# Decoder layer on one core: weights centred first, four weight sums on VectorE, a new order of the front

## The chip, the cores and the metric

The kernel runs on one core of one Trainium2 chip. The metric is the device time in microseconds (us) of one execution; lower is better. Engines are called as the profile calls them: PE (TensorE), DVE (VectorE), ACT (ScalarE), POOL (GpSimd) and SP (SyncE, which issues all DMAs here). A line such as L1070 is that line of the kernel's file.

## What is computed

One decoder layer over 8 sequences ("batches") of 512 tokens with 256 features, in float32. Three sublayers, each on a layer norm of x and added to x:

- A, self attention with one head of 128: softmax(Q Kᵀ / sqrt(128)) V, times a mask over the head's dimension, times w_o.
- B, cross attention with a context: relu(x̂ Wᵀ + b) against relu(ctx Wᵀ + b), masked keys out, softmax, times ctx.
- C, a gated FFN of 1024 with quantised products: activations are rounded to 8 bits per token, weights to -1, 0, 1 by the mean of |w| of each of the three matrices, out = down(silu(gate(x̂)) * up(x̂)).

The reference, cut:

```
x = x + attn(layernorm(x), head_dim_mask, w_q, w_k, w_v, w_o)
x = x + xattn(layernorm(x), ctx, mask, W, b)
scale = 1 / clip(mean(|w|), 1e-5);  w3 = clip(round(w * scale), -1, 1) / scale
x = x + bitlinear(silu(bitlinear(xn, w_gate)) * bitlinear(xn, w_up), w_down)
```

## The kernel before

Nothing loops over the work in order: five lists, PE_ORDER, ACT_ORDER, DVE_ORDER, POOL_ORDER and SP_ORDER, hold the steps of each engine one after the other, and every engine runs its list, each step waiting on counting semaphores for what it needs. An entry is stream.step/batch. Streams: W and F prepare weights (F those of the FFN), E is the context's projection (YP), A, B and C are the sublayers, S are loads and stores on SP. So a step that waits holds all that stand behind it in its engine's list, and a load that waits on SP holds the later loads.

Products are made in fp32r pieces: a tensor is split into a high part (a copy by ACT, `hi`) and a low part (source minus high part, by DVE or POOL, `lo`), and PE does hi*hi, hi*lo, lo*hi (product3, L1070 to L1072). Batch 0 of stream A uses plain float32 products instead, on copies of Q, K, V (L1080, L1125, L1139).

Steps of A for a batch: bn, ag (DVE: statistics of x), rs (POOL: reciprocal deviation), xT (ACT hi and POOL lo of the transposed x), Q, K, V (PE, then copies), VT (transposed V), S0 to S3 (scores of 128 queries; DVE multiplies them by the deviations and takes the maximum, L1479), N (its negative), exp (ACT, L867), P0 to P3 (PE transposes of the exponentials, copied as hi and lo), H (times V), Y0, Y1 (times w_o; DVE adds to x). Of batch 0 the deviations come through W.rs (DVE) and W.r (PE, then ACT's copy of r); DVE's V step (L1491) and S steps need that copy. From batch 1 on they go to DRAM and come back spread over the partitions (SP steps S.rw, S.rb).
The weights of Q, K, V are centred by their column means instead of centring x: W.sumQ/K/V on PE (L1317), then centreQ/K/V on DVE (L1614), in place; W.qkv (ACT) and W.split (DVE) make their hi and lo parts for batches 1 to 7.
Steps of B: norm (ACT), XT0, XT1 (PE transposes, hi on ACT, lo on DVE), XP0, XP1 (projection; relu on ACT, lo on POOL), S, exp, P, O (DVE adds to x), ctx (hi on ACT, lo on POOL), mask (ACT turns the loaded bytes into float, L905, which DVE adds to the scores).
Steps of C: bn, ag, rs, sh, norm, mx, sc, rc, xq (quantising; xq on POOL), S.xqT (a transposing DMA from SP), g0 to g7 and u0 to u7 (PE, L1284), t (ACT tanh), u (ACT copy), G (gate on DVE, product on POOL), hm, hs, hr, hq, hb, S.hT (transposing DMA), DN (PE, L1304).

The weights of the FFN are prepared once: F.gate, F.up, F.down load 1 MB each; F.sum0 to F.sum5 sum |w| over halves of gate (0, 1), up (2, 3), down (4, 5), all on ACT (L859, Abs with an accumulator); F.total (PE) adds over the partitions; F.sc0 to F.sc3 (DVE) make the scales; F.round (POOL) and F.sign (ACT) make the -1, 0, 1. B.XT1/0 waits for F.sc0, as they use one bank.

PSUM banks of stream A are dealt out by a_tables: each step of the front takes the next bank of a written list and waits until what was in it has been read. SECOND_BANKS are those of A_NEXT, the end of batch 1; from batch 2 on A takes a0 and a1 in turn and YP takes e.

Of the kernel before, what the change touches and what calls it, by code (L numbers as in the profile page):

```python
# [79 lines left out]
DVE_DN = [(n, t) for n in range(8) for t in range(4) if (n, t) not in POOL_DN]  # L80
SILU = [(6, j) for j in range(4, 8)] + [(7, j) for j in range(8)]
# [8 lines left out]
    E.YP1/3 A.Y0/2 A.Y1/2 C.g0/0 C.u0/0 A.Q/3 B.S0/1 B.S1/1 C.g1/0 C.u1/0 B.P0/1 B.S2/1 C.u2/0 C.g2/0 A.K/3  # L90
    A.V/3 B.P1/1 C.u3/0 C.g3/0 B.O0/1 B.S3/1 B.P2/1 C.g4/0 C.u4/0 E.YP0/4 C.g5/0 B.O1/1 C.u5/0 B.P3/1 B.O2/1
    A.VT/3 A.S0/3 B.O3/1 C.g6/0 C.u6/0 E.YP1/4 B.XT0/2 B.XT1/2 C.g7/0 C.DN0/0 C.u7/0 A.S1/3 A.P0/3 B.XP0/2
    B.XP1/2 A.S2/3 C.DN1/0 C.u0/1 C.g0/1 A.P1/3 A.S3/3 B.S0/2 B.S1/2 C.g1/1 C.u1/1 B.P0/2 B.S2/2 C.DN2/0 C.g2/1
    C.u2/1 C.DN3/0 B.P1/2 B.O0/2 A.P2/3 A.P3/3 C.g3/1 C.u3/1 B.S3/2 B.P2/2 C.g4/1 A.H/3 B.O1/2 B.P3/2 C.u4/1
# [1629 lines left out]
```

## Time and profile before

| | us |
|---|---|
| median of 3 runs | 372.09 |
| lowest and highest run | 371.5, 402.81 |
| the profiled execution | 372.06 |
| its span, first to last instruction | 370.1 |
| busy in it: PE, PEld, DVE, ACT, POOL | 361.5, 280.2, 313.8, 318.6, 294.0 |

The span is that of the instructions of one profiled execution; its own time has 1.96 us around them. In a timeline each row has start and length in us, engine, line, operation, the tile written and the tiles read, and the count where instructions are merged; brackets hold the idle time before it and what ended it. Matmuls overlap, so the start of the next one says more than the length.

### The profile page before, as it was taken

The numbers are of one execution on the slowest core, as the hardware profiler recorded it, in microseconds if no ns is written. First come the engines' busy times: TensorE is split into PE (matmuls) and PEld (weight loads), VectorE is DVE, ScalarE is ACT, GpSimd is POOL, SyncE is SP. The second block draws the span as 40 slices with busy tenths as digits, with TensorE's granted clock in tenths as the row PEclk, the third lists the DMA queues.
The fourth block names the chain that finished last, engine by engine and source line by source line (L and its number), as shares of the span: only waits on it lengthen the run. The fifth ranks groups of instructions, "written<-read, shape, count | busy, mean of one in ns | idle before, by whom it ended". The sixth has DMA issues, their size and how long they took to land.

```text
span 370.1 us, 7362 instructions
## 1 busy us (share of the span) xinstructions
PE 361.5 (98%) x2116; PEld 280.2 (76%) x2116; DVE 313.8 (85%) x918; ACT 318.6 (86%) x590; POOL 294.0 (79%) x421
## 2 busy tenths in 40 slices
...
DMA packets 47735, 36.92 MB, mean 100 GB/s; under 512 B 39248, under 2 KB 40912, under 8 KB 47312
## 3 DMA queue, kind: packets, MB, share of 16 engines
...
## 4 chain that ended last, share of the span: by engine, by line
PE 76%; POOL 6%; ACT 5%; DMA 4%; DVE 3%; issue 3%; SPq 1%; POOLq 0%; ACTq 0%; DVEq 0%
PE b_bank L1070 8%; PE b_bank L1071 8%; PE b_bank L1072 8%; PE a_bank L1070 6%; PE a_bank L1072 6%; PE a_bank L1071 6%; PE g_bank L1284 5%; PE d_bank L1304 5%; PE u_bank L1284 5%; PE b_bank L1212 3%; DMA x_all<-in_x 2%; PE a_bank L1132 2%; PE b_bank L1183 2%; POOL c_work L703 1%; POOL xp_lo L656 1%
## 5 line engine op out<-in xcount | busy, mean ns | idle before, releaser
L703 POOL TENSOR_TENSOR c_work<-c_work 128x512 f32<-128x512 f32 x48 | 61.8, 1297 | 3.4 <-DVE c_work L1540 2.4
L960 ACT ACTIVATE c_work<-g_bank,c_tanh_scale 128x512 f32<-128x512 f32 x52 | 35.9, 690 | 5.8 <-PE g_bank L1284 3.3
L1070 PE MATMUL b_bank<-ctx_hi,b_pT_hi 128*128 128x256 f32 x128 | 39.2, 307 | 0.0
L1540 DVE SCALAR_TENSOR_TENSOR c_work<-c_work,g_bank 128x512 f32<-128x512 f32 x50 | 33.9, 678 | 6.1 <-ACT c_work L960 5.7
L1071 PE MATMUL b_bank<-ctx_lo,b_pT_hi 128*128 128x256 f32 x128 | 36.1, 282 | 0.0
L1072 PE MATMUL b_bank<-ctx_hi,b_pT_lo 128*128 128x256 f32 x128 | 36.0, 282 | 0.0
L963 ACT ACTIVATE c_work<-u_bank 128x512 f32<-128x512 f32 x48 | 28.9, 601 | 8.2 <-PE u_bank L1284 8.2
L1284 PE MATMUL g_bank<-gateT,xqT 128*128 128x512 bf16 x112 | 33.6, 382 | 0.9 <-ACT xqT L935 0.5
L750 POOL TENSOR_SCALAR c_work<-c_work,h_q 128x1024 f32<-128x1024 f32 x28 | 31.7, 1132 | 3.2 <-DVE h_q L1574 3.2
L1284 PE MATMUL u_bank<-upT,xqT 128*128 128x512 bf16 x112 | 33.5, 381 | 0.6 <-DVE c_work L1535 0.6
L1567 DVE TENSOR_REDUCE h_max<-c_work 128x1 f32<-128x1024 f32 x26 | 31.4, 1206 | 1.1 <-POOL c_work L703 1.1
L1304 PE MATMUL d_bank<-downT,c_half 128*128 128x256 bf16 x240 | 31.2, 273 | 0.2 <-DMA c_half<-c_half 0.2
L1304 PEld LDWEIGHTS d_bank<-downT,c_half 128*128 128x128 bf16 x240 | 22.7, 98 | 8.5 <-issue 2.7
L651 POOL TENSOR_TENSOR yp_lo<-e_relu,yp_hi 128x512 fp32r<-128x512 f32 x16 | 20.7, 1295 | 10.2 <-ACT yp_hi L889 10.2
L970 ACT ACTIVATE c_half<-c_work 128x1024 bf16<-128x1024 f32 x26 | 27.3, 1056 | 0.5 <-POOL c_work L750 0.5
L1070 PE MATMUL b_bank<-yp_hi,xp_hi 128*128 128x512 f32 x64 | 27.4, 429 | 0.1
L1070 PEld LDWEIGHTS b_bank<-ctx_hi,b_pT_hi 128*128 128x128 f32 x128 | 24.3, 190 | 1.8 <-issue 0.2
L643 POOL TENSOR_TENSOR a_xT_lo<-a_xT_raw,a_xT_hi 128x512 fp32r<-128x512 f32 x14 | 18.4, 1316 | 8.6 <-ACT a_xT_hi L844 8.6
L1072 PE MATMUL b_bank<-yp_hi,xp_lo 128*128 128x512 f32 x64 | 25.2, 394 | 0.0
L898 ACT ACTIVATE b_p<-b_p,b_nmax 128x512 f32<-128x512 f32 x32 | 23.1, 723 | 2.5 <-DVE b_nmax L1516 2.4
L1071 PE MATMUL b_bank<-yp_lo,xp_hi 128*128 128x512 f32 x64 | 25.1, 391 | 0.0
L1516 DVE CUSTOM_DVE_ANT_0 b_p<-b_bank,mask_add 128x512 f32<-128x512 f32 x32 | 21.8, 683 | 3.7 <-PE b_bank L1072 3.6
...
## 6 DMA issues: line engine op xcount, KB each, us to landing
ctx_raw<-in_ctx SPq DMA_DIRECT2D x8, 512.0 KB, 4.5
a_xT_raw<-in_x_t SPq DMA_DIRECT2D x7, 512.0 KB, 4.4
ctxT_raw<-in_ctx_t SPq DMA_DIRECT2D x7, 512.0 KB, 5.4
x_all<-in_x SPq DMA_DIRECT2D x7, 512.0 KB, 3.8
out<-x_all SPq DMA_DIRECT2D x7, 512.0 KB, 2.9
...
c_work<-in_w_gate SPq DMA_DIRECT2D x1, 1024.0 KB, 10.9
c_work<-in_w_up SPq DMA_DIRECT2D x1, 1024.0 KB, 12.6
```

Of the source, the lines that this page charges most:

```text
L703: pool.tensor_tensor(h[:, t % 2, half * HALF:(half + 1) * HALF], th[:, j % 2, :], up[:, j % 2, :], ALU.mult).then_inc(hs, 1)
L750: pool.tensor_scalar(h_tile(t, n), h_tile(t, n), h_q[:, t:t + 1], ROUND if n < LAST else ROUND_F16, ALU.mult, ALU.add).then_inc(h_rounds, 1)
L960: act.activation(gate_tile(j, n), gu_bank("g", j, n), ACT.Silu if (n, j) in SILU else ACT.Tanh, scale=c_tanh_scale[:, j // 2:j // 2 + 1]). ...
L963: act.activation(up[:, j % 2, :], gu_bank("u", j, n), ACT.Copy).then_inc(ups, 1)
L970: act.activation(h_q8[:, t % 2, :], h_tile(t, n), ACT.Copy, bias=-ROUND).then_inc(hqs, 1)
L1070: pe.matmul(dst, l_hi, r_hi, start=first, stop=False)
L1071: pe.matmul(dst, l_hi, r_lo, start=False, stop=False)
L1072: return pe.matmul(dst, l_lo, r_hi, start=False, stop=last)
L1284: mm = pe.matmul(dst, xqT[:, t * DC + c, :], w[:, c, cols], start=c == 0, stop=c == DC - 1)
L1304: mm = pe.matmul(dn_bank(t, n)[:, 0:D], h_T[:, t % 2, f, :], downT[:, f, :], start=f == 0, stop=f == FC - 1)
L1540: dve.scalar_tensor_tensor(gate_tile(j, n), gate_tile(j, n), 1.0, gu_bank("g", j, n), ALU.add, ALU.mult).then_inc(gates, 1)
L1567: dve.tensor_reduce(h_max[:, one], h_tile(t, n), AX.X, ALU.max, apply_absolute_value=True).then_inc(h_maxes, 1)
```

## The change

1. On DVE all three centrings stand ahead of the statistics of batch 0; K's copy stands ahead of W.split and W.rs.
2. On PE A.S0/0 and A.S1/0 stand ahead of W.r, and E.YP1/0 directly behind E.YP0/0.
3. On SP the load of x of batch 1 goes ahead of W.o, xT/1 and ctxT/1; the mask of batch 0 is loaded behind all weights and S.rw/1, the mask of batch 1 behind S.xqT0/0 and S.ctxT/4. Other loads change places too.
4. F.sum2 to F.sum5 run on DVE (tensor_reduce of absolute values), with a semaphore of their own; ACT keeps F.sum0 and F.sum1.
5. Q and K of batch 2 ("batch three") run before P2 and P3 of batch 1 ("batch two") on PE, in banks e and b0.
6. The lists of all five engines are new up to about the middle of batch 0's FFN, and as before from there: A.S1/3 on PE, B.XT0/2 on ACT, A.N1/3 on DVE, C.G1/1 on POOL, S.hT1/0 on SP.

```diff
-A_NEXT = "S3/1 P1/1 P2/1 P3/1 H/1 Y0/1 Y1/1"
+A_NEXT = "S3/1 P1/1 Q/2 P2/1 K/2 P3/1 H/1 Y0/1 Y1/1"
...
-SECOND_BANKS = ["u", "d", "a0", "a1", "g", "u", "d"]
+SECOND_BANKS = ["u", "d", "e", "a0", "b0", "a1", "g", "u", "d"]
...
+    later = [entry for entry in later if entry not in A_NEXT.split()]
...
+DVE_SUMS = [2, 3, 4, 5]
+ACT_SUMS = [m for m in range(6) if m not in DVE_SUMS]
...
 PE_ORDER = """
-    W.sumQ/0 W.sumK/0 W.sumV/0 A.Q/0 A.K/0 A.V/0 W.r/0 E.YP0/0 A.S0/0 A.S1/0 A.VT/0 A.S2/0 A.S3/0 E.YP1/0 A.P0/0
-    A.P1/0 A.Q/1 A.P2/0 A.K/1 A.P3/0 A.V/1 E.YP0/1 A.H/0 A.VT/1 A.S0/1 A.S1/1 A.Y0/0 E.YP1/1 A.S2/1 A.P0/1
-    A.Y1/0 A.S3/1 A.P1/1 F.total/0 A.P2/1 A.P3/1 E.YP0/2 A.H/1 B.XT0/0 B.XT1/0 E.YP1/2 A.Y0/1 B.XP0/0 B.XP1/0
-    A.Y1/1 A.Q/2 A.K/2 B.S0/0 B.S1/0 A.V/2 B.P0/0 B.S2/0 A.VT/2 B.P1/0 A.S0/2 B.O0/0 B.S3/0 A.S1/2 B.P2/0 B.O1/0
...
+    W.sumQ/0 W.sumK/0 W.sumV/0 A.Q/0 A.K/0 A.V/0 A.S0/0 A.S1/0 W.r/0 E.YP0/0 E.YP1/0 A.VT/0 A.S2/0 A.S3/0 A.P0/0
+    A.P1/0 A.Q/1 A.P2/0 A.K/1 A.P3/0 A.V/1 E.YP0/1 A.H/0 A.VT/1 A.S0/1 A.S1/1 A.Y0/0 A.S2/1 E.YP1/1 A.P0/1
+    A.Y1/0 A.S3/1 A.P1/1 A.Q/2 A.P2/1 A.K/2 A.P3/1 F.total/0 E.YP0/2 A.H/1 B.XT0/0 B.XT1/0 E.YP1/2 B.XP0/0
+    B.XP1/0 A.Y0/1 A.Y1/1 A.V/2 B.S0/0 B.S1/0 A.VT/2 B.P0/0 B.S2/0 A.S0/2 B.P1/0 B.O0/0 A.S1/2 A.P0/2 B.S3/0
...
+    B.XP1/1 E.YP1/3 A.Y0/2 A.Y1/2 C.g0/0 C.u0/0 B.S0/1 B.S1/1 C.g1/0 C.u1/0 A.Q/3 B.P0/1 C.g2/0 C.u2/0 B.S2/1
...
 ACT_ORDER = """
-    A.Q/0 W.qkv/0 W.hi/0 A.xT0/1 E.ctxT/1 A.xT1/1 W.r/0 E.YP0/0 A.VT/0 W.wo/0 F.sum0/0 A.exp0/0 A.exp1/0
-    A.exp2/0 E.YP1/0 A.exp3/0 A.P0/0 A.Q/1 A.P2/0 A.K/1 F.sum1/0 F.sum2/0 E.YP0/1 A.xT0/2 A.xT1/2 F.sum3/0 A.H/0
-    A.VT/1 F.sum4/0 F.sum5/0 A.exp0/1 E.YP1/1 A.P0/1 E.ctxT/2 A.exp1/1 A.exp2/1 A.exp3/1 A.P1/1 A.P2/1 A.P3/1
-    B.mask/0 E.YP0/2 B.norm0/0 B.norm1/0 A.H/1 B.XT0/0 B.XT1/0 B.ctx/0 F.sign0/0 F.sign1/0 B.XP0/0 B.XP1/0
...
+    A.Q/0 W.qkv/0 W.hi/0 W.r/0 A.xT0/1 A.xT1/1 E.YP0/0 A.exp0/0 A.VT/0 A.exp1/0 E.ctxT/1 A.exp2/0 A.exp3/0
+    E.YP1/0 A.P0/0 A.Q/1 A.P2/0 A.K/1 W.wo/0 F.sum0/0 E.YP0/1 A.xT0/2 A.xT1/2 B.mask/0 A.H/0 A.VT/1 F.sum1/0
+    B.ctx/0 A.exp0/1 A.exp1/1 E.YP1/1 E.ctxT/2 A.exp2/1 A.P0/1 A.P1/1 A.Q/2 A.exp3/1 A.P2/1 A.K/2 A.P3/1
+    B.norm0/0 B.norm1/0 E.YP0/2 B.XT0/0 B.XT1/0 A.H/1 E.ctxT/3 B.XP0/0 B.XP1/0 F.sign0/0 F.sign1/0 F.sign2/0
...
+    B.XT1/1 E.YP0/3 F.sign4/0 F.sign5/0 A.H/2 B.XP0/1 B.XP1/1 C.norm1/0 B.ctx/1 B.mask/1 C.t0/0 E.ctxT/4 C.u0/0
...
 DVE_ORDER = """
-    W.centreQ/0 W.centreK/0 A.bn0/0 A.bn1/0 A.ag0/0 A.ag1/0 W.centreV/0 W.split/0 W.rs/0 A.K/0 W.lo/0 W.wo0/0
-    A.bn0/1 A.bn1/1 A.V/0 A.ag0/1 A.S0/0 A.S1/0 A.N0/0 A.N1/0 A.ag1/1 W.wo1/0 A.S2/0 A.S3/0 A.N2/0 A.N3/0
-    A.inv/0 A.P1/0 A.Q/1 A.K/1 A.P3/0 A.V/1 A.H/0 A.S0/1 A.N0/1 A.VT/1 A.S1/1 A.Y0/0 B.bn0/0 A.N1/1 A.S2/1
...
+    W.centreQ/0 W.centreK/0 W.centreV/0 A.bn0/0 A.bn1/0 A.ag0/0 A.ag1/0 A.K/0 W.split/0 W.rs/0 A.bn0/1 A.bn1/1
+    A.ag0/1 A.V/0 A.S0/0 A.S1/0 A.N0/0 W.lo/0 A.N1/0 W.wo0/0 A.ag1/1 A.S2/0 A.S3/0 A.N2/0 A.N3/0 F.sum2/0 A.P1/0
+    A.Q/1 A.K/1 A.P3/0 W.wo1/0 F.sum3/0 F.sum4/0 A.V/1 F.sum5/0 A.H/0 A.inv/0 A.S0/1 A.VT/1 A.N0/1 A.S1/1 A.N1/1
+    A.Y0/0 A.S2/1 A.N2/1 B.bn0/0 A.Y1/0 A.S3/1 B.ag0/0 B.bn1/0 A.N3/1 A.P0/1 A.P1/1 A.Q/2 B.ag1/0 A.P2/1 A.K/2
+    A.P3/1 B.sh0/0 B.sh1/0 A.bn0/2 A.bn1/2 A.ag0/2 A.ag1/2 A.bn0/3 F.sc0/0 F.sc1/0 F.sc2/0 F.sc3/0 A.inv/1
...
 SP_ORDER = """
-    W.qkv/0 W.t0/0 W.t1/0 W.x0/0 W.x1/0 W.o/0 W.W/0 W.c/0 S.xT/1 S.ctxT/1 S.mask/0 S.x/1 F.gate/0 F.up/0
-    F.down/0 S.rw/1 S.xT/2 S.rb/1 S.ctxT/2 S.x/2 S.x/3 S.mask/1 S.mask/2 S.ctx/0 S.rw/2 S.xT/3 S.rb/2 S.ctxT/3
-    S.rw/3 S.ctx/1 S.ctxT/4 S.xqT0/0 S.xqT1/0 S.xT/4 S.rb/3 S.ctx/2 S.ctxT/5 S.hT0/0 S.hT1/0 S.xqT0/1 S.hT2/0
...
+    W.qkv/0 W.t0/0 W.t1/0 W.x0/0 W.x1/0 W.W/0 W.c/0 S.x/1 W.o/0 S.xT/1 S.ctxT/1 F.gate/0 F.up/0 F.down/0 S.xT/2
+    S.rw/1 S.mask/0 S.ctx/0 S.rb/1 S.ctxT/2 S.x/2 S.x/3 S.ctxT/3 S.rw/2 S.rb/2 S.ctx/1 S.xT/3 S.xqT0/0 S.ctxT/4
+    S.mask/1 S.xqT1/0 S.rw/3 S.rb/3 S.ctx/2 S.ctxT/5 S.mask/2 S.hT0/0 S.xT/4 S.hT1/0 S.xqT0/1 S.hT2/0 S.hT3/0
...
@@ act @@
             def prep_sum(j):
                 act.wait_ge(ffn_loaded[j // 2], 16)
-                if j > 0:
-                    act.wait_ge(w_sums, j)
+                if ACT_SUMS.index(j) > 0:
+                    act.wait_ge(w_sums, ACT_SUMS.index(j))
...
@@ pe @@
-                    pe.wait_ge(w_sums, 6)
+                    pe.wait_ge(w_sums, len(ACT_SUMS))
+                    pe.wait_ge(dve_w_sums, len(DVE_SUMS))
...
@@ dve @@
+            def prep_sum(j):
+                dve.wait_ge(ffn_loaded[j // 2], 16)
+                dve.tensor_reduce(w_sum[:, j % 2, j // 2:j // 2 + 1], ffn_raw[j // 2][:, (j % 2) * F:(j % 2 + 1) * F], AX.X, ALU.add,
+                                  apply_absolute_value=True).then_inc(dve_w_sums, 1)
```

## Rows read from the trace of the kernel before

**Rows 1.** The page, part 1: busy time, share of the span, instructions
```profile
...
PE 361.5 (98%) x2116; PEld 280.2 (76%) x2116; DVE 313.8 (85%) x918; ACT 318.6 (86%) x590; POOL 294.0 (79%) x421
...
```

**Rows 2.** Waits of PE, 0 to 50: us in total, times, longest
```profile
...
PE d_bank L1132 <- ACT a_p L867: 1.1, 1, 1.1
PE u_bank L1116 <- DVE vT L1491: 1.0, 1, 1.0
...
PE b_bank L1322 <- DVE vT L1367: 0.5, 1, 0.5
PE g_bank L1070 <- DVE a_pT_lo L1464: 0.4, 1, 0.4
```

**Rows 3.** Windows: length, busy us by engine, clock, DMA share, GB/s
```profile
...
10.00:20.00 10.00, 8.50 (x23) 3.51 (x22) 7.50 (x22) 6.46 (x13) 7.20 (x8) 1.00 1.02 419
...
43.50:86.00 42.50, 42.45 (x245) 36.68 (x246) 31.44 (x110) 37.17 (x68) 30.84 (x38) 1.00 0.27 74
...
340.00:370.10 30.10, 25.98 (x201) 17.63 (x199) 25.27 (x69) 25.61 (x45) 22.82 (x48) 1.00 0.38 106
...
```

**Rows 4.** Timeline of DVE, 0 to 50
```profile
...
8.82 0.46 DVE L1614 SCALAR_TENSOR_TENSOR b_p<-u_bank,b_p 128x128 f32<-128x128 f32 x2
...
11.66 0.68 DVE L1450 COPY upT<-a_bank 128x512 f32<-128x512 f32 x1
...
15.32 1.41 DVE L1355 BATCH_NORM_STATS2 a_bn<-x_all 128x6 f32<-128x256 f32 x4 [2.31 <-DMA x_all<-in_x]
...
32.88 0.69 DVE L1468 TENSOR_TENSOR hT_lo<-d_bank,hT_hi 128x512 fp32r<-128x512 f32 x1 [4.57 <-ACT hT_hi L838]
...
```

**Rows 5.** Chain that ended last, 6 to 16: start us, us, what
```profile
...
6.19 9.11 DMA x_all<-in_x
...
```

**Rows 6.** Tile mask_u, 0 to 50: its loads, issue to landing
```profile
...
DMA to landing us min/median/max: 3.4/3.7/7.9
```

**Rows 7.** Timeline of PE: start, length in us, instruction, idle before
```profile
...
22.09 0.48 PE L1070 MATMUL d_bank<-a_xT_hi,wqkv_hi 128*128 128x512 f32 x1
...
23.56 0.60 PE L1132 MATMUL a_bank<-ident,a_p 128*128 128x128 f32 x4
...
28.61 3.60 PE L1139 MATMUL d_bank<-x_all,downT 128*128 128x512 f32 x8
...
39.74 0.63 PE L1132 MATMUL d_bank<-ident,a_p 128*128 128x128 f32 x4 [1.05 <-ACT a_p L867]
...
43.55 0.47 PE L1070 MATMUL g_bank<-a_pT_hi,b_pT_hi 128*128 128x512 f32 x1 [0.38 <-DVE a_pT_lo L1464]
...
85.80 0.60 PE L1284 MATMUL g_bank<-gateT,xqT 128*128 128x512 bf16 x2
...
```

**Rows 8.** Timeline of ACT, 25 to 50
```profile
...
34.46 1.06 ACT L859 ACTIVATE gateT<-c_half 128x1024 f32<-128x1024 f32 x1
...
35.52 0.71 ACT L867 ACTIVATE a_p<-a_p,a_nmax 128x512 f32<-128x512 f32 x1
...
36.22 0.67 ACT L888 ACTIVATE e_relu<-a_bank,wo_and_small 128x512 f32<-128x512 f32 x1
...
37.36 0.59 ACT L831 ACTIVATE a_pT_hi<-a_bank 128x512 fp32r<-128x512 f32 x1
37.84 1.06 ACT L919 ACTIVATE ctxT_hi<-ctxT_raw 128x1024 fp32r<-128x1024 f32 x1
38.79 0.72 ACT L867 ACTIVATE a_p<-a_p,a_nmax 128x512 f32<-128x512 f32 x1
...
```

**Rows 9.** Groups of DVE by form: count, busy us, mean ns, idle before
```profile
...
L1567 DVE TENSOR_REDUCE h_max<-c_work 128x1 f32<-128x1024 f32 x26 | 31.4, 1206 | 1.1 <-POOL c_work L703 1.1
...
```

**Rows 10.** The page, part 6: DMA issues, KB each, us to landing
```profile
...
ctxT_raw<-in_ctx_t SPq DMA_DIRECT2D x7, 512.0 KB, 5.4
...
c_work<-in_w_up SPq DMA_DIRECT2D x1, 1024.0 KB, 12.6
```

**Rows 11.** Timeline of SP, 0 to 60
```profile
...
5.70 0.44 SPq L550 DMA_DIRECT2D mask_u<-in_mask  x1
...
```

More of the change, by code:

```diff
@@ L90 @@
[L90 to L94, printed above, removed]
```

222 lines of the change are left out of this document (112 added, 110 removed).

## The prediction

> **What bounds the kernel now.** I read the page first: TensorE (PE) is busy for 361.5 of 370.1 us [rows 1]. So only PE's idle time can be won, unless its work shrinks, and the change leaves every matmul and transpose in place. Next, the waits of PE: in the front part four stand out, 1.1 us for an exponential of ACT, 1.0 and 0.5 us for VectorE (DVE) at vT, 0.4 us for a DVE low half [rows 2]. By stretch, the granted clock is 1.00 [rows 3], the upper level (2.4 GHz), so no clock is to be won; PE is busy 42.45 of 42.5 us from 43.5 to 86, while the last 30 us hold 4.1 us of idle time [rows 3] that no edit here touches. The orders of all engines are the same from about the middle of batch 0's FFN on. So the change plays in the first 110 us, and what it can win is 0.5 + 1.0 + 1.05 + 0.4 = 2.9 us.
>
> The profiled execution took 372.06 us (span 370.1 and 1.96 around it); the median of the runs is 372.09, so a difference to the span carries over to the median as it stands.
>
> **Part 1, start to 20 us: 0.5 + 1.0 us.** The W.r matmul waited 0.5 us for DVE's W.rs [rows 2], since S0 and S1 of batch 0 stood behind it. They need only the copies of Q and K. K's copy started at 11.66 [rows 4], behind the centring of V, a split and W.rs. Now centreV is first: it ran at 8.82 behind the statistics [rows 4] but PE has its sum by 6, so it fits at 6.1 and costs nothing (0.46 us in idle DVE time). K's copy then follows the statistics and runs when PE has K, at 9.4 to 10.1. PE goes from A.V (ends about 11.2) into S0, S1 (0.86 us each, 13.0), and W.rs, done near 11.7, is ready for W.r. The 0.5 us go.
> The 1.0 us stood before A.VT: DVE multiplied V only after the statistics of batch 1, which began at 15.32 [rows 4] because x of batch 1 took 9.11 us from issue at 6.19 [rows 5]. Its load now goes ahead of W.o, xT, ctxT and the mask: issue about 4.2, and 1.2 MB less ahead of it. At the 419 GB/s of the stretch from 10 to 20 us [rows 3] that is about 2.9 us earlier, 12.4. Bounds: 7.6 at best (3.4 us to landing, the shortest of [rows 6]) to 15.3 (no gain). W.r ends 13.9, ACT's copy of r 14.5, V's product 15.2; VT is due on PE at 17.4, behind YP0, YP1. Statistics (1.41 us [rows 4]) may start as late as 13.0 and cost nothing. Started at 15.3 they would let V's product end at 17.5, while YP1/0 needs V's bank free at 15.7: 1.8 us lost, more than is won here. I take the full 1.5 us. The loads that fall behind x/1 (W.o, xT/1, ctxT/1) have users at 14.5 and later.
> H of batch 0 starts at 28.61 now [rows 7], so at 27.1.
>
> **Part 2, the sums.** Four of six sums of |w| go from ACT to DVE. On ACT one occupies 1.06 us (start at 34.46, next instruction at 35.52) [rows 8]: 4.2 us off ACT. On DVE no row shows this sum; the nearest is the largest |h| over the same 128x1024, 1206 ns [rows 9]. Above, four statistics over 1024 elements in all took 1.41 [rows 4]; below, 0.68 for a DVE copy of 512 [rows 4]. I take 1.21, so 4.8 us on DVE. The cover: DVE idles 4.57 us before the low half of H/0 at 32.88 [rows 4]. New queue: sum2 at 20.6 (up landed at 20.2 before, 12.6 us [rows 10] after its issue at 7.6; P1/0's copy waits behind it until 22.4, due by V/1 at 24.2); P3's copy ends 26.9; then wo1, sum3, sum4 to 29.7, V/1's product 30.3 (VT/1 due 30.6), sum5 31.5, H's low half 32.1 (Y0/0 due 32.4). All covered, by 0.3 us: this is the thinnest cover of the front, and at 1.41 each it is 0.3 us short.
>
> **Part 3, Q/2 and K/2 ahead of P2/1 and P3/1: 1.05 + 0.4 us.** From H/0 to the end of S3/1 PE is dense: 28.61 to about 38.7 [rows 7], hence 27.1 to 37.2 after. Then it waited 1.05 us for exp1 until 39.74 [rows 7], as exp0 had stood behind two sums till 35.52 [rows 8]. Pitches on ACT, start to start: exp 0.70, relu pair 1.14, copy 0.48, ctxT 0.95 [rows 8]. After: H and VT copied 31.6, sum1 32.7, B.ctx/0 (moved up) 33.6, exp0 at 33.7 (DVE's maximum is then there), exp1 34.5 to 35.2, due at 37.2. Hidden. Then YP1/1 36.4, ctxT/2 37.4, exp2 38.1, P0, P1 39.1, Q/2 39.7, exp3 40.4, P2 40.9, K/2 41.5, P3 42.0. On PE P1/1 ends at 37.7, Q/2 takes 1.47 us (22.09 to 23.56 [rows 7]) to 39.1, P2/1 finds exp2 done, K/2 to 41.0, P3/1 finds exp3 done with 0.6 us to spare. F.total and YP0/2 (0.4 + 1.6) fill the time till DVE's last low half at 42.8; H/1 is due at 43.5. Before, it started at 43.55 [rows 7] without the 2.9 us of Q/2 and K/2; so PE is 2.9 us ahead there. The banks e and b0 that Q/2 and K/2 take are read at 40.9 and 42.2, before YP0/2 (due 41.8) and XT0 (due 46.3).
>
> **Part 4, what is late next.** XP0/0 now stands ahead of Y0/1 and Y1/1, so 1.4 us of its cover is gone: shifts 43.3, two norms 45.3, YP0/2's relu 46.4, XT0 and XT1 copied by 47.8, low halves 48.6, due 48.65. Nothing to spare; DVE has the statistics of batches 2 and 3 and all four F.sc steps ahead of these halves (to 46.7). I allow 0.2 to 0.3 us here, 0.1 in part 2, and 0.2 for C.g1/C.u1 below: 0.6 in all. S0/0 follows at 54.3, its POOL halves are ready at 53.9.
> B.mask/0 moved: its load is not needed till S0/0. B.mask/1, though, is now issued behind the transposing DMA xqT0/0 and ctxT/4, and ACT's mask step stands ahead of C.t0/0. With 2.3 to 2.9 us gained, g0 (85.80 now [rows 7]) is at about 83.0. xq0 is ready at 77.0, so the mask is issued at 78.7. Mask loads took 3.4 to 7.9 us [rows 6]; the 7.9 is the one issued at 5.70 [rows 11], behind half-megabyte loads. A ctxT load takes 5.4 us [rows 10], so by the rows either 3.7 us (82.4) or, behind ctxT/4, 84.0. Needed: u1 on PE at 87.0 waits for u0's copy, which comes 2.7 us behind the mask (mask, tanh, ctxT/4, copy), so 84.3. It just holds.
 By the rule the mask is at 84.0 and my sum stands; without it at 82.4, and the 0.2 us allowed there fall away.
>
> **Sum.** 2.9 - 0.6 = 2.3 us: 372.06 - 2.3 = 369.8. From part 4 to the end every engine keeps its order and PE is dense, so the lead carries through.
>
> **Rivals.** (a) All covers hold: 2.9 us, 369.1. For it: pitches, not durations, set the queues. Against it: three places with under 0.3 us to spare. Chance 0.15.
> (b) DVE takes over as the bound: its queue from 26.9 to 32.2 and from 42 to 48.6 is full. If the sums take 1.41 us and each hand-over 0.1 more, PE loses 0.3 + 1.0: about 371.0. For it: 4.8 us more work in 28 us. Against: 4.57 us idle before. Chance 0.17.
> (c) The mask: one 64 KB load holds ACT, and with it tanh 0, gate 0 and g1/u1. Each us past 84.3 costs one. At 7.9 us (86.6) the gain is gone, 372.1; that is the point from which it decides. At 9.11, the longest landing of the front [rows 5], it is at 87.8, a loss of 3.5: 372.06 - 2.3 + 3.5 = 373.3, slower than before. For it: the transposing DMA and 512 KB stand ahead. Against: little else moves then. Chance 0.12.
> (d) The change doesn't deliver: the waits vanish but return further back, where the old orders start (the load of xT for batch 4 now waits behind hT0/0): 372. Chance 0.08.
> My forecast has 0.48; its own range is 369.2 to 370.6.
>
> **Numbers.** 369.8 us, range 368.6 to 373.1: below, (a) less 0.5 for the scatter of the runs (the two lower ones are 0.6 apart); above, up to just short of the worst of (c). A measurement of this kernel tells about 2% (7.4 us) from no change. Faster by more would need more idle time than the front has: 0.01. Slower by more needs 9.7 us on top of the forecast, nearly three times the 3.5 of (c): 0.03 for what I don't see. Within: 0.96.
>
> **What would show it.** Right: PE's waits for a_p (1.1), vT (1.0, 0.5) gone; H/0 at 27.1, H/1 near 43.5 with Q/2 and K/2 done; the DVE sums 1.2 us each, between 20 and 32; g0 near 83.2. Wrong: a wait of PE on hT_lo or b_T_lo over 0.5 us (b), ACT idle before mask_add near 84 and PE idle at g or u (c), a lead at 86 that is gone at 123 (d), or x/1 landing after 14.

## The result and the profile after

The changed kernel takes 369.56 us (median of 4 runs, 369.08 to 369.96), the kernel before took 371.79 (median of 4): ratio 0.993, 95% interval 0.9909 to 0.9951. A second series of the same kernel (a1 below) gave 369.53 against 371.82, ratio 0.9933. So the time fell by 2.2 to 2.3 us; that is clear of the noise and within 2%. A ratio here is the record's estimate with its interval, not the quotient of two medians (for e4 below 1.006, where the medians give 1.008). One run of the kernel before (402.81 us) and one of e6 (452.52 us) stand far above the other runs of their kernel; the ratios leave such runs out, the medians do not. The profiled execution of the changed kernel took 369.78 us, its span 367.8.

The page's part 1 and the waits of PE from 0 to 50 us, changed kernel. Some of PE's records are missing here (2089 of 2116), so its busy sum is not compared.

```profile
PE 359.3 (98%) x2089; PEld 279.1 (76%) x2116; DVE 318.6 (87%) x922; ACT 313.9 (85%) x582; POOL 293.0 (80%) x421
```

```profile
PE b_bank L1311 <- POOL ones L628: 1.0, 1, 1.0
PE b_bank L1072 <- DVE b_T_lo L1513: 0.3, 1, 0.3
```

All four waits of [rows 2] are gone. What is left ahead of 50 us is the start itself and 0.3 us at XP0/0. DVE gained 4.8 us of busy time and ACT lost 4.7, as four sums moved from the one to the other should.

PE's timeline, changed kernel: start, length, instruction. The rows are A.Q/0, H/0, P1/1, Q/2, P2/1, K/2, P3/1, H/1, XP0/0 and g0/0.

```profile
5.22 1.02 PE L1082 MATMUL a_bank<-c_xn,b_p 128*128 128x512 f32 x2
...
25.93 3.60 PE L1141 MATMUL d_bank<-x_all,downT 128*128 128x512 f32 x8
...
35.83 0.60 PE L1134 MATMUL d_bank<-ident,a_p 128*128 128x128 f32 x4
36.19 0.48 PE L1072 MATMUL e_bank<-a_xT_hi,wqkv_hi 128*128 128x512 f32 x1
37.66 0.60 PE L1134 MATMUL a_bank<-ident,a_p 128*128 128x128 f32 x4
38.02 0.48 PE L1072 MATMUL b_bank<-a_xT_hi,wqkv_hi 128*128 128x512 f32 x1
39.51 0.60 PE L1134 MATMUL a_bank<-ident,a_p 128*128 128x128 f32 x4
41.82 0.47 PE L1072 MATMUL g_bank<-a_pT_hi,b_pT_hi 128*128 128x512 f32 x1
47.39 0.47 PE L1072 MATMUL b_bank<-b_T_hi,wt_hi 128*128 128x512 f32 x1 [0.27 <-DVE b_T_lo L1513]
...
82.36 0.38 PE L1286 MATMUL g_bank<-gateT,xqT 128*128 128x512 bf16 x1
```

From H/0 to H/1 no row of PE shows idle time. Against [rows 7] H/0 is 2.68 us earlier, P1/1 3.91, H/1 1.73 with Q/2 and K/2 (1.47 us each) already done, which makes 4.67, and g0/0 is 3.44 earlier.

Two things in these leads are not the change's. First, A.Q/0 started at 5.22 here and at 5.90 in the profile before, while the first matmul of the sums of w_qkv started at 3.81 and 3.88. The second profile of the same kernel has

```profile
6.34 1.02 PE L1082 MATMUL a_bank<-c_xn,b_p 128*128 128x512 f32 x2
```

so this start moves by over 1 us between executions of one kernel; over 14 profiles of both orders it lies from 5.22 to 6.45. I therefore count from A.Q/0 to the end of the span. In that measure, called "length" below where it runs to the end of the span, the leads are 2.0 us at H/0, 4.0 at H/1, 2.8 at g0/0 (5.22 against 5.90 taken off), 3.0 at the second down projection (116.68 against 120.40), and only 1.6 at the end: 362.58 against 364.2 us.

The measure has a limit. In the ten profiles that have the changed kernel's start (all but the kernel before and e3, e6 and e9 below) H/0 stands 20.66 to 20.71 us behind A.Q/0. In the kernel before it does not hang on A.Q/0 but on x/1, which landed at 15.30, 13.3 us ahead of H/0 at 28.61; in e9, with the same late load, at 15.01, 13.4 us ahead of 28.37. So a profile of the old start with an early A.Q/0 has a longer length for nothing. The 5.90 of the profile before is close to the mean of the others, so the 364.2 is a fair base, to some 0.4 us either way (an estimate: e9 began A.Q/0 0.55 us earlier and is 0.35 us longer).

Second, the place where the lead falls. These are rows of SP, DVE and PE in the changed kernel: the store of batch 3's output and the load of batch 7's x into the same buffer, the statistics of that x, the low half of H/6 behind them, and Y0/6.

```profile
256.61 0.34 SPq L577 DMA_DIRECT2D out<-x_all  x1
261.49 0.33 SPq L514 DMA_DIRECT2D x_all<-in_x  x1
...
265.55 0.75 DVE L1358 BATCH_NORM_STATS2 a_bn<-x_all 128x6 f32<-128x256 f32 x2 [2.06 <-DMA x_all<-in_x]
...
267.14 0.68 DVE L1471 TENSOR_TENSOR hT_lo<-a_bank,hT_hi 128x512 fp32r<-128x512 f32 x1
...
267.96 0.35 PE L1072 MATMUL a_bank<-wo_hi,hT_hi 128*128 128x256 f32 x1 [0.96 <-DVE hT_lo L1471]
```

The load is issued when the store has landed: 4.88 us behind the store here, 2.69 in the profile before. DVE stands idle 2.06 us, and PE 0.96 us by the idle column, 1.2 by start to start: the lead over the kernel before, the 0.68 us of the start not taken off, goes from 3.73 to 2.55 us.

The sums and the mask: DVE, then SP and ACT, changed kernel.

```profile
8.86 0.69 DVE L1453 COPY upT<-a_bank 128x512 f32<-128x512 f32 x1 [0.42 <-PE a_bank L1082]
11.35 1.41 DVE L1358 BATCH_NORM_STATS2 a_bn<-x_all 128x6 f32<-128x256 f32 x4 [0.34 <-DMA x_all<-in_x]
...
19.64 1.21 DVE L1595 TENSOR_REDUCE w_sum<-c_work 128x1 f32<-128x1024 f32 x1
...
28.74 1.21 DVE L1595 TENSOR_REDUCE w_sum<-c_half 128x1 f32<-128x1024 f32 x1
30.19 0.69 DVE L1471 TENSOR_TENSOR hT_lo<-d_bank,hT_hi 128x512 fp32r<-128x512 f32 x1 [0.24 <-ACT hT_hi L840]
```

```profile
78.76 0.42 SPq L552 DMA_DIRECT2D mask_u<-in_mask  x1
...
82.62 0.62 ACT L907 ACTIVATE mask_add<-mask_u 128x512 f32<-128x512 uint8 x1
83.14 0.68 ACT L962 ACTIVATE c_work<-g_bank,c_tanh_scale 128x512 f32<-128x512 f32 x1
83.71 1.06 ACT L921 ACTIVATE ctxT_hi<-ctxT_raw 128x1024 fp32r<-128x1024 f32 x1
```

K's copy runs before the statistics of batch 1, these start as x/1 lands, the last sum ends 0.24 us ahead of H's low half, and ACT reached the mask step without idle time. The issues of ctxT/4 (at 78.19) and mask/1 (at 78.76) by their tiles, 78 to 86 us:

```profile
DMA to landing us min/median/max: 3.7/3.7/3.7
DMA to landing us min/median/max: 3.3/3.3/3.3
```

So ctxT/4 landed at 81.9 and mask/1 at 82.1, just behind it and 0.5 us before ACT came for it.

### The profile page after: what moved, and what is told of

Read it like the earlier page. It is cut to its first block, busy times and chain, and to the rows that moved or that the text cites. A ratio compares the mean times of both kernels' runs of the same rounds, so it can differ in the third digit from the quotient of the medians.

```text
span 367.8 us, 7327 instructions
## 1 busy us (share of the span) xinstructions
PE 359.3 (98%) x2089; PEld 279.1 (76%) x2116; DVE 318.6 (87%) x922; ACT 313.9 (85%) x582; POOL 293.0 (80%) x421
## 4 chain that ended last, share of the span: by engine, by line
PE 78%; POOL 6%; issue 4%; DMA 4%; ACT 4%; DVE 2%; POOLq 0%; ACTq 0%; DVEq 0%; SPq 0%
PE b_bank L1072 8%; PE b_bank L1073 8%; PE b_bank L1074 8%; PE a_bank L1072 6%; PE a_bank L1074 6%; PE a_bank L1073 5%; PE d_bank L1306 5%; PE g_bank L1286 5%; PE u_bank L1286 5%; PE b_bank L1214 3%; PE a_bank L1134 2%; POOL c_work L705 2%; PE b_bank L1185 1%; POOL xp_lo L658 1%; PE e_bank L1072 1%
## 5 line engine op out<-in xcount | busy, mean ns | idle before, releaser
L1286 PE MATMUL u_bank<-upT,xqT 128*128 128x512 bf16 x101 | 31.1, 381 | 1.2 <-DVE c_work L1538 0.6
L1286 PE MATMUL g_bank<-gateT,xqT 128*128 128x512 bf16 x96 | 30.1, 381 | 1.9 <-ACT xqT L937 0.5
L653 POOL TENSOR_TENSOR yp_lo<-e_relu,yp_hi 128x512 fp32r<-128x512 f32 x16 | 20.6, 1290 | 8.2 <-ACT yp_hi L891 8.2
L1073 PEld LDWEIGHTS b_bank<-ctx_lo,b_pT_hi 128*128 128x128 f32 x128 | 24.4, 190 | 0.5
L878 ACT ACTIVATE b_pT_hi<-b_bank 128x512 fp32r<-128x512 f32 x32 | 19.1, 596 | 6.6 <-PE b_bank L1214 6.2
```

What stands on the lines that cost most here:

```text
L1073: pe.matmul(dst, l_hi, r_lo, start=False, stop=False)
L1286: mm = pe.matmul(dst, xqT[:, t * DC + c, :], w[:, c, cols], start=c == 0, stop=c == DC - 1)
```

## The experiments

All are timed against the kernel before in the same series; the median of before was 371.82 to 371.89 in each. "Length" is from A.Q/0 to the end of the profiled span (before 364.2, changed 362.58); "by pitch" means by the distance between the starts of matmuls, against the usual distance.

**a1, the changed kernel again.**

> The changed kernel itself once more, for a second profile and more runs. Theory (two spots of PE's time differ from one execution to the next, whatever the orders: the six sums of w_qkv at the start, after which A.Q/0 began between 5.22 and 6.45 us in six profiles, and the store of batch 3's output with the load of batch 7's x behind it, 2.7 to 4.9 us from the issue of the one to the issue of the other): the median is 369.3 to 370.0, ratio 0.993 to 0.995, and in this profile the length from A.Q/0 to the end of the span is 361.4 to 362.6 us (364.2 in the kernel before), at the lower end if the store takes under 3 us. Rival (the early start of A.Q/0 at 5.22 belongs to the new order of loads and of the centring): A.Q/0 starts at 5.1 to 5.3 again.

Measured: 369.53 us, ratio 0.9933 (0.9907 to 0.9959); A.Q/0 at 6.34, so the early start is not the order's. Length 362.46 with a slow store again: x/7 issued 4.66 us behind the store, PE waited 0.5 us for hT_lo.

**e3 and e9, two pieces of part 1 alone, in the kernel before.** In e3 the load of W.o stays ahead of x/1. Neither has the new order of ACT.

```diff
 SP   (e3)  ... W.W/0 W.c/0 +S.x/1 S.xT/1 S.ctxT/1 S.mask/0 -S.x/1 ...
 DVE  (e9)  W.centreQ/0 W.centreK/0 +W.centreV/0 A.bn0/0 ... A.ag1/0 +A.K/0 -W.centreV/0 W.split/0 W.rs/0 -A.K/0 ...
 PE   (e9)  ... A.V/0 +A.S0/0 +A.S1/0 W.r/0 E.YP0/0 -A.S0/0 -A.S1/0 ...
```

> The kernel before with one move: the load of x for batch 1 is issued ahead of xT, ctxT and the mask instead of behind them. Theory (the idle time before VT/0 is that load's, and a shift of VT moves PE and ACT alike): VT/0 loses its wait of 1.2 us by start pitch, and the 1.0 to 1.2 us stay to the end: 370.7 to 370.9, ratio 0.997. W.r's wait stays. Rival (ACT, dense from 18 to 43 us in the kernel before, takes it back): PE's wait for exp1 at P1/1 grows from 1.2 to 2.3 us and the time stays 371.8 to 372.0, ratio 0.999 to 1.000.

> The kernel before with the other half of part 1 alone: V's columns centred ahead of the statistics, K's copy ahead of the split, S0/0 and S1/0 on PE ahead of W.r; the load of x for batch 1 stays late. Theory (the two waits of the front stand in one chain: V's product waits for the statistics of the late x/1 until 16.7 whatever PE did before): the 0.75 us in front of W.r go, the wait in front of VT/0 grows from 1.2 to 1.9 us by start pitch, and nothing is gained: 371.7 to 372.0, ratio 0.999 to 1.001. Rival (the prediction's sum, 0.5 + 1.0, with terms that can be had one by one): 0.5 to 0.75 us gained, ratio 0.998, and H/0 of batch 0 is 0.75 us earlier counted from A.Q/0.

Measured: e3 371.38 us, ratio 0.9988 (0.9975 to 1.0002), span 369.5; e9 372.63 us, ratio 1.0025 (1.0008 to 1.0042), span 369.9, against 370.1 for the kernel before. The waits of PE, e3 and then e9:

```profile
PE u_bank L1116 <- DVE vT L1491: 0.7, 1, 0.7
```

```profile
PE u_bank L1116 <- DVE vT L1491: 1.8, 1, 1.8
PE d_bank L1132 <- ACT a_p L867: 1.1, 1, 1.1
```

In e9 the wait in front of W.r is gone and the one at VT/0 has grown from 1.0 to 1.8 us; the seven of its 12 runs with a mean clock of 0.999 or 1.0 have a median of 371.89, the same as the kernel before (the other five come back under e5). In e3 x/1 landed at 11.21, but DVE's product with V waits for something else, ACT's copy of r:

```profile
15.96 0.69 DVE L1491 TENSOR_TENSOR vT<-g_bank,r_bc 128x512 f32<-128x512 f32 x1 [2.10 <-ACT r_bc L848]
```

```profile
12.46 0.63 ACT L844 ACTIVATE a_xT_hi<-a_xT_raw 128x512 fp32r<-128x512 f32 x1 [2.24 <-DMA a_xT_raw<-in_x_t]
13.80 1.06 ACT L919 ACTIVATE ctxT_hi<-ctxT_raw 128x1024 fp32r<-128x1024 f32 x1 [0.71 <-DMA ctxT_raw<-in_ctx_t]
...
15.28 0.58 ACT L848 ACTIVATE r_bc<-b_bank 128x512 f32<-128x512 f32 x1
```

PE had gone on from W.r to the next product at 12.46. The copy came 2.8 us later because ACT's list has xT/1 and ctxT/1 ahead of it and waits for their loads. So VT/0 has two suppliers, x/1 through the statistics, and r through ACT's queue. What takes the second out of the way is the new order of ACT (W.r/0 ahead of A.xT0/1, E.ctxT/1 behind A.exp1/0): in the changed kernel the copy ran at 13.15. Neither run here has it and none tries it alone, so its share isn't measured. H/0 is at 28.19 in e3, 0.42 us earlier than before, and that is what the medians show (0.45); e3 lies between its theory and its rival. (Its length, 363.05, would say 1.15, but A.Q/0 came at 6.45 in this profile, 0.55 us later than before, without H/0 coming later for it.)

**e6, the load of x/1 back, in the changed kernel.** `S.x/1` behind `S.ctxT/1`.

> The changed kernel with the load of x for batch 1 back behind xT/1 and ctxT/1 (issued near 5.7 instead of 4.0 us, with 1.3 MB more ahead of it), and nothing else undone: VectorE's statistics of batch 1 now stand ahead of V's product, where the kernel before had other work. Theory (the bound of the prediction): the load lands between 13.5 and 15.3, the statistics end 1.4 us later, V's product by 15.8 to 17.5, and PE loses 0 to 1.8 us at YP1/0 or VT/0, most likely 1.0: 370.0 to 371.4, ratio 0.995 to 0.998. Rival (the new order has spare time for it): no wait in PE before 20 us, as the changed kernel.

Measured: 370.49 us, ratio 0.9959 (0.9941 to 0.9978), 0.96 above a1, the size that the theory had. DVE and then the waits of PE:

```profile
13.61 1.41 DVE L1358 BATCH_NORM_STATS2 a_bn<-x_all 128x6 f32<-128x256 f32 x4 [2.14 <-DMA x_all<-in_x]
```

```profile
PE a_bank L1118 <- DVE vT L1494: 0.9, 1, 0.9
PE g_bank L1166 <- DVE vT L1494: 0.5, 1, 0.5
```

The 0.5 us are YP1/0, waiting for V's bank: x/1 landed at 13.59, 0.6 us past the 13.0 from which the prediction let it cost, and H/0 is 0.75 us later behind A.Q/0. The 0.9 us stand at VT/1, behind the late landing of rb/1 (30.68), a spot that e5 shows too and that is not part of the undone step. So the move itself explains some 0.75 us of this profile.

**e2, the sums back on ACT (part 2 undone).**

```diff
-DVE_SUMS = [2, 3, 4, 5]
+DVE_SUMS = []
 ACT  ... F.sum0/0 +F.sum1/0 +F.sum2/0 E.YP0/1 A.xT0/2 A.xT1/2 +F.sum3/0 ... A.VT/1 -F.sum1/0 +F.sum4/0 +F.sum5/0 B.ctx/0 A.exp0/1 ...
```

> The changed kernel with part 2 undone: all six sums of |w| on ACT, two behind W.wo's first sum, one behind the rounding of xT/2, two behind VT/1, as they stood before; all other orders stay. Theory (ACT was the bound of the front from 18 to 43 us): four sums are 4.2 us, of which the idle 0.44 and 0.61 us of ACT ahead of YP0/1 and H/0 take 1.0; exp1 of batch 1, now ended at 33.9, ends near 37.2 and P1/1, due at 35.83, waits 1.3 us or more; Y0/0 waits up to 1.8 us for H/0's halves. PE loses 1.5 to 2.5 us: 371.0 to 372.0 in all, ratio 0.998 to 1.000, that is most of the gain gone. Rival (the sums were covered by PE's own length, and the gain came from the other parts): at most 0.3 us lost, 369.5 to 369.9.

Measured: 372.32 us, ratio 1.0009 (0.9995 to 1.0024). The rest of the change without part 2 gains nothing. The waits of PE from 20 to 42 us:

```profile
PE u_bank L1072 <- issue: 1.9, 1, 1.9
PE a_bank L1134 <- ACT a_p L869: 0.7, 1, 0.7
```

Y0/0 and P1/1 wait where the theory said. The price was 2.8 us against a1, above its 1.5 to 2.5: the two waits add up to 2.6 where I had taken the first as partly covering the second.

**e4 and e5, Q/2 and K/2 back behind Y1/1 (part 3 undone).** They differ in ACT's queue: e4 copies Q/2 and K/2 behind the signs of W, e5 ahead of them.

```diff
-A_NEXT = "S3/1 P1/1 Q/2 P2/1 K/2 P3/1 H/1 Y0/1 Y1/1"
+A_NEXT = "S3/1 P1/1 P2/1 P3/1 H/1 Y0/1 Y1/1"
-SECOND_BANKS = ["u", "d", "e", "a0", "b0", "a1", "g", "u", "d"]
+SECOND_BANKS = ["u", "d", "a0", "a1", "g", "u", "d"]
 PE   ... A.P1/1 +F.total/0 -A.Q/2 A.P2/1 -A.K/2 A.P3/1 -F.total/0 ... A.Y0/1 A.Y1/1 +A.Q/2 +A.K/2 A.V/2 ...
```

> The changed kernel with part 3 undone: Q/2 and K/2 stand behind Y1/1 again on PE, ACT and VectorE, with the banks of before, and F.total between P1/1 and P2/1. Theory (Q/2 and K/2 give exp2 and exp3 of batch 1 their time): P2/1 waits 0.3 to 0.6 us for exp2 (ends near 36.9) and P3/1 about 1 us for exp3; the changed kernel's lead shrinks by 1.0 to 1.6 us, 370.6 to 371.2, ratio 0.996 to 0.998. Rival (with the sums off ACT the exponentials are early enough anyway): no more than 0.3 us lost, 369.5 to 369.9, ratio 0.993 to 0.994.

> As e4_qk2_back, part 3 undone, but on ACT the copies of Q/2 and K/2 stand ahead of the three signs of W, not behind them (there the 3.3 us of signs made V/2 on PE wait 1.5 us for q_lo, which is no cost of part 3). Theory: the waits for exp2 and exp3 stay (0.5 and 1.0 us in e4), the wait for q_lo goes: from A.Q/0 on 1.3 to 2.2 us more than the changed kernel, 370.9 to 371.8, ratio 0.997 to 1.000. Rival (Q/2 and K/2 are missing in front, whatever the signs do): 372.5 or more, ratio above 1.001.

Measured: e4 374.91 us, ratio 1.006 (1.0032 to 1.0088); e5 372.82 us, ratio 1.001 (0.9988 to 1.0033). The waits of PE from 20 to 70 us, e4 and e5:

```profile
PE a_bank L1134 <- ACT a_p L869: 1.5, 2, 1.0
PE a_bank L1072 <- DVE q_lo L1463: 1.5, 1, 1.5
```

```profile
PE a_bank L1134 <- ACT a_p L869: 1.5, 2, 1.0
PE a_bank L1118 <- DVE vT L1494: 1.0, 1, 1.0
```

Both show the waits for exp2 and exp3, 0.5 and 1.0 us; e4's third was my own doing and is gone in e5. The 1.0 us at VT/1 of e5 is no part of the undone step; DVE's row says what it is:

```profile
30.34 0.69 DVE L1494 TENSOR_TENSOR vT<-u_bank,r_bc 128x512 f32<-128x512 f32 x1 [1.41 <-DMA r_bc<-r_rows]
```

The medians are above both expectations, and the mean granted clock of each run goes with that. Of e5's 12 runs six, at 372.79 to 373.85 us, had a mean clock of 0.995; of the six at 0.999 or 1.0 four took 371.14 to 371.44 us (and two 373.0 and 373.3). So half the runs were some 2 us longer at a lower mean clock (0.995 over 370 us is 3.7 us at the half level, 1.8 us lost, by estimate); at full clock e5 is mostly in the theory's 370.9 to 371.8. e4 (4 of 7, the other three 372.56, 372.57 and 374.01) and e9 (5 of 12) have such runs too; a1, e1, e7, e10 and e11 have none in 37.

**e1, the statistics of x/7 later.** `A.bn0/7 A.ag0/7 A.bn1/7` on DVE behind `B.O1/5`.

> The changed kernel with one thing moved: VectorE's statistics of batch 7 (three steps) stand behind the low halves of H/6 and P2/5 instead of ahead of them. Theory (the lead is lost at the load of x for batch 7): in the changed kernel the load landed 4.0 us after its issue at 261.5, VectorE stood idle 2.06 us for it, and PE waited 0.96 us for hT_lo at 268, where the lead over the kernel before fell from 3.73 to 2.55 us. With the statistics behind the low half PE has no wait there, the lead stays near 3.7 us to the end: 368.4 us, ratio to before 0.990 to 0.991. Rival (a slow landing of one profiled execution, not of the others): median as the changed kernel, 369.4 to 369.7, ratio 0.993 to 0.994. Second rival (the lost time only comes back at the next dependence, ACT's or DVE's queue of batch 5): no wait at 268 but the lead is back to 2.5 us by 300.

Measured: 370.7 us, ratio 0.9965 (0.9946 to 0.9983), 1.2 us above a1. Its store took 2.70 us and PE had no wait at 268, but 4 us further on

```profile
PE a_bank L1072 <- DVE x_all L1501: 0.2, 1, 0.2
```

and the length, 362.34, is 1.0 us above that of e7 and e10. By pitch that wait is 0.5 us against e10, and another 0.4 follows at 275.6. The second rival came closest: where the statistics stood, DVE had waited 1.9 us for ACT anyway; behind the low half they pushed the work after them.

**e7, the store of batch 3 in two.**

```diff
 SP   ... S.xqT1/4 S.ctxT/7 +S.head/3 S.store/3 S.x/7 ...
...
-                    sp.dma_start(out[:, n], x_all[:, n % X_SLOTS]).then_inc(out_stored, 16)
+                    first = T - 1 if n == 3 else 0
+                    sp.dma_start(out[:, n, first:T], x_all[:, n % X_SLOTS, first:T]).then_inc(out_stored, 16)
...
```

> The changed kernel with the store of batch 3's output split: rows of tiles 0 to 2 are stored behind ctxT/7, tile 3 when it is ready, so that only 128 KB instead of 512 KB stand between the last addition and the load of x for batch 7. Theory (the lead is lost at this chain when the store is slow): the load of x/7 is issued 1.9 to 2.5 us behind the last addition instead of 2.7 to 4.9, PE's wait for hT_lo near 268 does not occur, and the median falls by the average of that wait, 0.2 to 1.0 us: 368.6 to 369.4, ratio 0.990 to 0.993. Rival (the stall was rare, or the time comes back behind it): no wait at 268 and the same median as the changed kernel within 0.2 us. Second rival (two stores in flight are no faster): x/7 issued as late as before.

Measured: 369.3 us, ratio 0.9932 (0.9911 to 0.9953). SP's rows (256.79 is the 128 KB store), and DVE's statistics of x/7, for which it no longer waits:

```profile
254.50 0.42 SPq L582 DMA_DIRECT2D out<-x_all  x1
256.79 0.34 SPq L578 DMA_DIRECT2D out<-x_all  x1
259.79 0.34 SPq L514 DMA_DIRECT2D x_all<-in_x  x1
```

```profile
263.59 0.75 DVE L1365 BATCH_NORM_STATS2 a_bn<-x_all 128x6 f32<-128x256 f32 x2
```

PE has no wait at 268 and the length is 361.26, 2.9 us under the kernel before. That is the whole lead of the front carried to the end. But the issue of x/7 came 3.0 us behind the store, not 1.9 to 2.5 (in e11, with the same split, 3.9), and the median is only 0.2 us under a1's: not told apart.

**e8, mask/1 ten microseconds late.** `S.mask/1` behind `S.xqT1/0`.

> The changed kernel with the load of mask/1 issued behind the second transposing DMA of batch 0 (xqT1/0) instead of behind ctxT/4: issue near 88.7 instead of 78.8 us, landing 3.4 to 5 us later, 92.1 to 93.7. Theory (the prediction's rival on the mask, its price: ACT's mask step stands ahead of C.t0/0, and each microsecond past 84.3 costs PE one): PE stands idle for a g or u bank near 87 and the time is 369.5 + 7.8 to 9.4, that is 377 to 379, ratio 1.015 to 1.020. Rival (ACT catches up out of its own idle time, and the order list lets PE run ahead): 373 to 375, ratio 1.003 to 1.009. If neither PE idle time nor time is added, the mask was never near the path.

Measured (two runs): 379.03 us, ratio 1.0193 (1.0175 to 1.021): the theory's price. ACT, PE, and the windows of PE (length; PE, PEld, DVE, ACT, POOL busy; granted clock; DMA share; GB/s):

```profile
93.02 0.63 ACT L907 ACTIVATE mask_add<-mask_u 128x512 f32<-128x512 uint8 x1 [9.34 <-DMA mask_u<-in_mask]
```

```profile
95.01 1.03 PE L1286 MATMUL g_bank<-gateT,xqT 128*128 128x512 bf16 x2 [8.12 <-DVE c_work L1543]
```

```profile
90.00:92.00 2.00, 0.00 (x0) 0.00 (x0) 0.00 (x0) 0.00 (x0) 0.00 (x0) 0.78 0.23 47
92.00:94.00 2.00, 0.00 (x0) 0.00 (x0) 0.00 (x0) 0.98 (x2) 0.00 (x0) 0.50 0.05 9
94.00:96.00 2.00, 0.99 (x3) 0.38 (x4) 1.74 (x4) 2.00 (x4) 0.19 (x1) 0.50 0.81 32
96.00:98.00 2.00, 2.00 (x7) 1.35 (x5) 1.97 (x9) 2.00 (x5) 1.81 (x3) 0.51 0.95 339
98.00:100.00 2.00, 2.00 (x13) 1.43 (x12) 0.62 (x3) 0.93 (x4) 1.43 (x2) 1.00 0.06 23
```

PE stood idle for 8.1 us, in which the granted clock fell, and then ran at the lower level (0.50, that is 1.2 GHz) from its restart at 95.0 to 98, which cost about 1.4 us more (by the pitch of starts against the changed kernel, 8.3 and then 1.4). With 1 us lost per us of delay, as priced, the mask decides from 93.02 - 8.3 = 84.7 us, in the time of this profile whose g0 came 0.7 later than the changed kernel's: 84.0 in that one's time. One run can't tell this point and the slope apart; that the priced slope puts the point within 0.3 us of the text's 84.3 speaks for both.

**e10, mask/0 and ctx/0 out of rb/1's way; e11, three moves together.** e10 moves `S.mask/0 S.ctx/0` behind `F.down/0`. e11 adds e7's store and

```diff
-A_NEXT = "S3/1 P1/1 Q/2 P2/1 K/2 P3/1 H/1 Y0/1 Y1/1"
+A_NEXT = "S3/1 P1/1 Q/2 P2/1 K/2 P3/1 H/1 V/2 Y0/1 Y1/1"
 PE   ... E.YP1/2 +A.V/2 B.XP0/0 B.XP1/0 A.Y0/1 A.Y1/1 -A.V/2 B.S0/0 ...
```

> The changed kernel with the loads of mask/0 and ctx/0 issued behind the load of W_down, at about 8.7 us, instead of between the store and the load of the row of 1/std of batch 1 (rw/1 and rb/1). In the profiles of the changed order that load, issued at 22.6 to 23.6, let V's product of batch 1 begin on VectorE at 28.1 to 30.3, where it waited 0, 0.58 and 1.41 us for it; in the worst one PE waited 0.97 us at VT/1. Theory (the 577 KB of mask/0 and ctx/0 stand in rb/1's way): no wait of VectorE for r_bc over 0.1 us in this profile, and the median falls by the average of the waits, 0.2 to 0.6 us against a1: 369.0 to 369.4, ratio 0.991 to 0.993. Rival (the landing scatters by itself, mask and ctx have no part): the same median as the changed kernel, and r_bc waited for as often. Second rival (the early loads delay W_up and W_down): VectorE waits for the landing of W_down at its second or third sum.

> The changed kernel with three moves together: the store of batch 3 in two (e7), mask/0 and ctx/0 ahead (e10), and V/2 on PE ahead of XP0/0, with bank a1, instead of behind Y1/1, so that 1.4 us of matmuls cover ACT's and VectorE's halves of XT1/0. Theory: the waits for r_bc, for x/7 (hT_lo near 268) and for b_T_lo near 47 (0.4 us by start pitch) all go; from A.Q/0 to the end of the span 360.6 to 361.0 us (361.26 in e7, 362.5 in the two profiles of the changed kernel), median 368.4 to 369.0, ratio 0.990 to 0.992, faster than both kernels. Rival (Y0/1, Y1/1 1.4 us later make the statistics of batch 1 late for S0/0 and XT0/1): a new wait between 47 and 72 us gives the 0.4 us back and the median is 369.3 or more.

Measured: e10 369.56 us, ratio 0.9932 (0.9919 to 0.9946), length 361.3, no wait for r_bc and none of PE at 268; the median is a1's. The load rb/1 itself was quick, 3.9 us, and 4.0 in e11 with the same loads, against 3.9 to 7.6 in the other nine profiles of the new order of loads. But the row's store took 5.0 us before rb/1 could be issued (24.86 instead of 22.4 to 23.6), and 5.8 in e11, against 2.9 to 4.5. From the issue of the store to the landing of rb/1 it took 8.9 and 9.8 us, and 8.5 to 10.8 in the other nine: the delay moved from the load to the store, and in e11 DVE waited 0.46 us for r_bc again. So the median goes with the rival, but its reason, a landing that scatters by itself, is half the story: with the old order of loads (before, e3, e9) the pair took 7.1 to 7.2 us each time. What in the new order makes it slower isn't shown. e11 370.61 us, ratio 0.9964 (0.9951 to 0.9977), 1.1 us above a1. The wait at XP0/0 was gone, and this one had come, at S0/0:

```profile
PE b_bank L1079 <- POOL xp_lo L665: 1.3, 1, 1.3
```

V/2 had covered POOL's halves of XP0 and XP1; 1.4 us of cover taken from one place were missing at the next. The place is the rival's (between 47 and 72 us), its supplier is not: the rival had DVE's statistics late, and it was POOL. No version here is faster than the changed kernel by what these runs can tell.

## Why the prediction was right, and where it was not

The forecast was 369.8 us, by a sum of 2.3 us; measured 2.2 to 2.3, median 369.56. The sum came out, its parts did less well, and that they cancel is in part luck.

- **Part 1** was given 1.5 us and measured 2.0 at H/0, counted from A.Q/0. The mechanism was as told: K's copy early, x/1 landing at about 11.3 (forecast 12.4, 7.3 us from issue), V's product 1.3 us ahead of the forecast 15.2. What was mis-sized is the term itself. The idle column counts to the modelled end of the matmul before; by the pitch of starts the two waits were 0.75 (11.05 to 11.80) and 1.17 us, 1.9 together. And the two terms had a condition that the text used without naming it: ACT's copy of r right behind W.r (its 14.5), which takes the new order of ACT. e3 shows what happens without it: x/1 lands early, and VT/0 still waits 0.8 us by pitch. e9 shows that the 0.5 us at W.r alone gives nothing.
- **Part 2** did what was forecast: 1.21 us per sum, the first at 19.64 (20.6), H's low half at 30.19 (32.1, with PE 1.2 us earlier than forecast). Its cover held. e2 gives its worth, 2.8 us, which the prediction booked nowhere: it had it inside the 1.05 us of part 3. Without it the other parts' gain is gone.
- **Part 3**: 1.05 + 0.4 forecast; by pitch 1.22 + 0.54, and the lead grew from 2.0 to 4.0 us between H/0 and H/1, of which 0.2 is not in these terms. The order of ACT was right: exp1 from 33.2 (forecast 34.5), exp2 from 36.3, exp3 from 38.4, each ahead of its transposes. e5 takes the step back and finds the waits for exp2 and exp3, 0.5 and 1.0 us.
- **Part 4**: XP0/0 waited 0.27 us by the idle column, 0.43 by pitch (0.2 to 0.3 allowed). With the same work between them the lead fell from 4.0 us at H/1 to 2.8 at g0/0, though: 0.25 more by pitch at P0/0 (56.57), 0.23 at g0/0, 0.09 at S0/0 and the rest in smaller pieces, none of which the idle column shows. The mask, landed at 82.1, cost nothing (0.2 allowed), and e8 fits the deciding point of 84.3, plus the clock. By the ring order of the Trainium skill, DMA: Bandwidth & Descriptors, section "Queues, rings and completion order", the text put the mask behind ctxT/4, at 84.0. (The section also says that completion is not first in, first out for an issuing engine, so it promises no such landing.) Here the trace agrees with the order, 82.1 behind 81.9; what was wrong is the 5.4 us taken for ctxT/4, a median over loads of which this one took 3.7.
- **"From part 4 to the end every engine keeps its order and PE is dense, so the lead carries through"** is the step that failed. It carried to 267, then the profile gave 1.2 us back at x/7, where PE had not been on a chain of DMAs in the profile before. Store and load moved together by 3.7 us, so the lead alone doesn't put one in the other's way. From the issue of batch 3's store to that of x/7 it took 2.7 us in the profile before and in e1, e2 and e9, and 3.7 to 4.9 in the changed kernel (twice), e3, e4, e5, e6, e8 and e10, kernels of either order. e4 and e5, slow, had no lead there, and e1, quick, had all of it; but the other three quick ones had none, so that the lead has no part in it is likely and not shown. With the 0.6 allowed this cancelled the under-sized terms, so the 2.3 came out for a reason partly not its own.
- **Rivals.** (a) is nearest for the trace: 2.9 us in the executions without a wait at x/7 (e7, e10). (b) did not occur, and e11 shows how close it is, on POOL. (c) was real in mechanism and price, and not reached, by 1.9 us (82.1 against 84.0). (d) had the kind of loss right, one that returns late, and the wrong place.
- The gain is 2.9 us in length where no DMA is late (to some 0.4, as said above), and 2.25 in the medians. The stall at x/7 takes part of the difference. rb/1's landing (0 to 1.0 us of PE's time, only in the new order of loads, whose pair of store and load is 1.3 us slower or more) may be the rest; e10 did not mend it, and how much it costs the median stays open.
